# Moving the second stage's input normalization of 14 of 16 images out of the first stage, in a two-stage convolution kernel

## The reference, cut to what matters

```
x = x + L0_conv(gn(x))   # gn: each channel of each image to mean 0, variance 1
x = x + L1_conv(gn(x))
```

## Time and profile before

| | |
|---|---|
| median of 3 runs | 2269.34 us (2268.66 to 2269.86) |
| the profiled execution | 2273.27 us, of which the span of the profile is 2271.2 us |
| PE busy | 2145.7 us, 94% of the span |
| DVE, ACT, POOL busy | 77%, 63%, 23% |
| bytes moved by DMA | 248.21 MB, mean 109 GB/s |
| chain that ended last | 90% PE, 4% issue, 2% ACT, 2% DVE, 1% DMA |

### The profile page before, as it was taken

How to read it: one execution, slowest core, us unless ns; L and a number is a source line. 1 busy time by engine, 2 the same in 40 slices (tenths; PEclk the granted TensorE clock), 3 DMA queues, 4 the chain that set the end, 5 groups by cost and what they waited for, 6 DMA issues and landing times.

```text
span 2271.2 us, 101012 instructions
## 1 busy us (share of the span) xinstructions
PE 2145.7 (94%) x45303; PEld 1364.8 (60%) x45303; DVE 1741.6 (77%) x4186; ACT 1432.6 (63%) x2629; POOL 517.1 (23%) x323
## 2 busy tenths in 40 slices
PE   6888888977999999999999999999999999999997
PEld 3333333336666666666666666666666666666664
DVE  4666666645888888888888888788888888878886
ACT  3456655656666666666666666666666666666662
POOL 1000000000332222322222222233322322322222
PEclk9989988888999999999999999999999999999998
DMA  7688888876333333333333333333433333333312
GB/s 144 163 220 224 223 219 219 207 193 157 79 83 84 79 90 86 79 78 79 79 79 81 85 83 79 83 88 79 97 85 82 88 79 88 79 78 79 79 40 57
DMA packets 60386, 248.21 MB, mean 109 GB/s; under 512 B 12393, under 2 KB 12658, under 8 KB 53810
## 3 DMA queue, kind: packets, MB, share of 16 engines
q1 hardware_dynamic: 59954, 241.75, 44.9%
HBM read 139.99 MB, written 101.72 MB: 106 GB/s over the span
## 4 chain that ended last, share of the span: by engine, by line
PE 90%; issue 4%; ACT 2%; DVE 2%; DMA 1%; POOL 0%; SPq 0%; POOLq 0%; ACTq 0%
PE bank L590 24%; PE bank L530 17%; PE bank L575 10%; PE bank L662 10%; PE bank L650 9%; PE bank L603 7%; PE bank L683 6%; PE bank L612 5%; DVE arena L1215 2%; ACT arena L826 1%; ACT arena L731 1%; DMA arena<-tap_rows_in 1%; PE bank L544 0%; ACT arena L817 0%; PE bank L492 0%
## 5 line engine op out<-in xcount | busy, mean ns | idle before, releaser
L459 POOL TENSOR_TENSOR arena<-arena 128x8 f32<-128x8 f32 x256 | 492.8, 1925 | 1238.0 <-DVE arena L1125 1235.5
L590 PE MATMUL bank<-arena 128*64 128x512 f16 x4608 | 690.2, 394 | 0.0
L817 ACT ACTIVATE arena<-bank 100x512 f32<-100x512 f32 x1024 | 581.8, 599 | 110.1 <-PE bank L575 79.4
L575 PEld LDWEIGHTS bank<-arena 128*64 128x64 f16 (+1 forms) x8192 | 328.7, 104 | 232.6 <-issue 22.3
L530 PE MATMUL bank<-arena 32*32 32x508 f32 (+1 forms) x9216 | 384.2, 655 | 51.1 <-issue 36.4
L575 PE MATMUL bank<-arena 128*64 128x128 f16 (+1 forms) x8192 | 389.3, 220 | 18.0 <-DVE arena L1109 11.5
L1215 DVE TENSOR_TENSOR arena<-bank,arena 128x512 f32<-128x512 f32 x512 | 328.9, 684 | 48.2 <-issue 44.9
L826 ACT ACTIVATE arena<-bank,arena 128x256 f32<-128x256 f32 x512 | 261.3, 561 | 114.1 <-PE bank L603 111.2
L859 ACT ACTIVATE arena<-bank 128x512 f32<-128x512 f32 x256 | 152.9, 597 | 225.7 <-PE bank L650 223.9
L1144 DVE TENSOR_TENSOR arena<-arena,bank 128x512 f32<-128x512 f32 x256 | 174.8, 683 | 139.6 <-ACT arena L826 139.6
L650 PE MATMUL bank<-arena 100*32 100x128 f32 x8192 | 276.1, 275 | 1.3 <-ACT arena L817 1.3
(11 more groups left out here) (113 smaller groups left out, 1655.9 us busy)
## 6 DMA issues: line engine op xcount, KB each, us to landing
arena<-xn_d SPq DMA_DIRECT2D x128, 536.2 KB, 4.8
xn_d<-arena SPq DMA_DIRECT2D x130, 260.0 KB, 4.4
x_d<-arena SPq DMA_DIRECT2D x64, 512.0 KB, 8.1
arena<-x_d SPq DMA_DIRECT2D x128, 256.0 KB, 4.1
out<-arena SPq DMA_DIRECT2D x128, 256.0 KB, 2.7
arena<-x_in SPq DMA_DIRECT2D x32, 544.0 KB, 9.6
arena<-x_in SPq DMA_DIRECT2D x32, 528.0 KB, 9.4
arena<-spectra_in SPq DMA_DIRECT2D x1, 384.0 KB
```

The lines of the kernel that those rows point to most:

```text
L459: pool.tensor_tensor(tiny["rstd"][:, slot], tiny["var_eps"][:, slot], powers, ALU.pow).then_inc(s_root, 1)
L575: mm = pe.matmul(ring[g % len(ring)][low:high, 128 * i:128 * i + 128], w[:, first + low:first + high], hidden_w, start=True, stop=True)
L590: mm = pe.matmul(v_banks[chunk % 3][64 * s:64 * s + 64, :], v_w[:, 64 * tap:64 * tap + 64], at(xs[u % 3], row * WP + 32 * k + dx, [32 * WP ...
L817: act.activation(h_rows[0:WIN, :, first:first + 4], ring[g % len(ring)][0:WIN, :].rearrange("p (i c) -> p c i", i=4), ACT.Copy).then_inc(s ...
```

## The change

- **First stage.** Only images 0 and 1 (`EARLY`) are still normalized and stored to `xn_d` here. An image of `x` is loaded in eight DMAs of about 270 KB in place of four, `x2` is stored in eight of 256 KB in place of four of 512 KB, and each waits for a step of the convolution (`s_conv_step`): an x piece at steps 0, 2, ... 14, an x2 piece at steps 1, 3, ... 15. The `xs` of units 0 and 1 are loaded during the convolutions of images 14 and 15.
- **Second stage.** The other 14 images are normalized by halves: in units 0 to 27, `load_half` brings back rows of `x2_d`, ACT normalizes (`norm_half`) and rounds (`high_half`) within `spectral`, DVE computes the lost part (`low_half`), and `store_half` writes `xn_d`, two units ahead of the load that reads it. `xs` has two buffers, not three, and is loaded in two parts: rows 0 to 41 (`load_top`, four DMAs of 341 KB, each waited for) and rows 42 to 65 (`load_bottom`, four DMAs of 195 KB, waited for in pairs). `load_res` comes first in SP's unit and waits for each pair.

```diff
+    EARLY = 2
+    TOP = 42
+    HALVES = 2 * (NB - EARLY)
...
-            def load_x(b, quarters):
+            def load_x(b, part, q):
                 flat = x[b].rearrange("c h w -> c (h w)")
-                for q in quarters:
-                    first, last = max(q * (H // Q) - 1, 0), min((q + 1) * (H // Q) + 1, H)
-                    at_row = first - (q * (H // Q) - 1)
-                    sp.dma_start(xq[b % 3][32 * q:32 * q + 32, at_row * W:(at_row + last - first) * W],
-                                 flat[:, first * W:last * W]).then_inc(s_x_in[b % 3], 16)
-            def store_x2(b):
-                rows = x2_d[b].rearrange("ch (r c e) -> ch r c e", r=4, c=4)
-                for c in range(4):
-                    sp.dma_start(rows[:, :, c, :], x2[b % 3][32 * c:32 * c + 32, :].rearrange("p (r e) -> p r e", r=4)).then_inc(
-                        s_x2_out[b % 3], 16)
-            def store_xn(b):
-                for part, buf in ((0, xh), (1, xl)):
-                    rows = xn_d[b, part, :, 1:H + 1, :].rearrange("ch (r c y) w -> ch r c (y w)", r=4, c=4)
-                    for c in range(4):
-                        sp.dma_start(rows[:, :, c, :], buf[32 * c:32 * c + 32, :].rearrange("p (r e) -> p r e", r=4)).then_inc(
-                            s_xn_out, 16)
+                band_top, half_band = q * (H // Q) - 1, BAND // 2
+                first, last = max(band_top + half_band * part, 0), min(band_top + half_band * (part + 1), H)
+                sp.dma_start(xq[b % 3][32 * q:32 * q + 32, (first - band_top) * W:(last - band_top) * W],
+                             flat[:, first * W:last * W]).then_inc((s_x_first_in, s_x_second_in)[part][b % 3], 16)
+            def store_x2(b, c, half):
+                rows = x2_d[b].rearrange("ch (r c e) -> ch r c e", r=4, c=4)[:, 2 * half:2 * half + 2, c, :]
+                sp.dma_start(rows, x2[b % 3][32 * c:32 * c + 32, QPIX // 2 * half:QPIX // 2 * (half + 1)].rearrange(
+                    "p (r e) -> p r e", r=2)).then_inc(s_x2_out[b % 3], 16)
+            def store_xn(b, part, c):
+                rows = xn_d[b, part, :, 1:H + 1, :].rearrange("ch (r c y) w -> ch r c (y w)", r=4, c=4)
+                sp.dma_start(rows[:, :, c, :], (xh, xl)[part][32 * c:32 * c + 32, :].rearrange("p (r e) -> p r e", r=4)).then_inc(
+                    s_xn_out, 16)
...
-            def load_xs(u, paced=True):
-                b, half = divmod(u, 2)
+            def load_band(u, landed, first, last, g):
+                b, h = divmod(u, 2)
+                src = xn_d[b, g % 2, :, h * (H // 2) + first:h * (H // 2) + last, :].rearrange("c h w -> c (h w)")
+                sp.dma_start(xs[u % 2][32 * g:32 * g + 32, first * WP:last * WP], src).then_inc(landed[u % 2], 16)
+            def load_xs(u, landed, first, last, at_once):
                 for g in range(4):
-                    src = xn_d[b, g % 2, :, half * (H // 2):half * (H // 2) + HALF, :].rearrange("c h w -> c (h w)")
-                    sp.dma_start(xs[u % 3][32 * g:32 * g + 32, :], src).then_inc(s_xs_in[u % 3], 16)
-                    if paced:
-                        sp.wait_ge(s_xs_in[u % 3], 64 * (u // 3) + 16 * (g + 1))
+                    load_band(u, landed, first, last, g)
+                    if (g + 1) % at_once == 0:
+                        sp.wait_ge(landed[u % 2], 64 * (u // 2) + 16 * (g + 1))
+            def load_top(u, at_once):
+                load_xs(u, s_top_in, 0, TOP, at_once)
+            def load_bottom(u, at_once):
+                load_xs(u, s_bottom_in, TOP, HALF, at_once)
...
                 older, prev, later = image(b - 2), image(b - 1), image(b + 2)
-                if later is not None:
-                    if b > 0:
-                        sp.wait_ge(s_conv_mm, NCH * b)
-                    load_x(later, (0, 1))
-                if prev is not None:
-                    sp.wait_ge(s_x2_ready, NCH * b)
-                    store_x2(prev)
-                if later is not None:
-                    load_x(later, (2, 3))
-                if b == NB + 1:
-                    load_xs(1, paced=False)
-                if older is not None:
-                    sp.wait_ge(s_xl_ready, 4 * (older + 1))
-                    store_xn(older)
-                if b == NB - 3:
-                    sp.wait_ge(s_xn_out, 128 * (older + 1))
+                if b == NB - 2:
+                    sp.wait_ge(s_xn_out, 128)
                     sp.wait_ge(s_pads_stored, 32)
-                    load_xs(0, paced=False)
+                for piece in range(8):
+                    if 0 <= b < NB:
+                        sp.wait_ge(s_conv_step, 18 * b + 2 * piece + 1)
+                    if later is not None:
+                        if piece == 0 and b > 0:
+                            sp.wait_ge(s_conv_mm, NCH * b)
+                        load_x(later, piece // 4, piece % 4)
+                    if NB - 2 <= b < NB:
+                        u = b - NB + 2
+                        if piece < 4:
+                            load_band(u, s_top_in, 0, TOP, piece)
+                        else:
+                            load_band(u, s_bottom_in, TOP, HALF, piece - 4)
+                    if 0 <= b < NB:
+                        sp.wait_ge(s_conv_step, 18 * b + 2 * piece + 2)
+                    if prev is not None:
+                        if piece == 0:
+                            sp.wait_ge(s_x2_ready, NCH * b)
+                        store_x2(prev, piece % 4, piece // 4)
+                    if older is not None and older < EARLY:
+                        if piece == 0:
+                            sp.wait_ge(s_xh_ready, 2 * (older + 1))
+                        if piece == 4:
+                            sp.wait_ge(s_xl_ready, 4 * (older + 1))
+                        store_xn(older, piece // 4, piece % 4)
...
-            def load_res(u, pair):
-                for s in range(2):
-                    p0 = 64 * pair + 32 * s
-                    sp.dma_start(res[p0:p0 + 32, :].rearrange("p (l r) -> p l r", l=2),
+            def load_res(u):
+                for part in range(4):
+                    pair, s = divmod(part, 2)
+                    sp.dma_start(res[32 * part:32 * part + 32, :].rearrange("p (l r) -> p l r", l=2),
                                  image_rows(x2_d, u // 2, u % 2, pair, s)).then_inc(s_res_in, 16)
+                    if s == 1:
+                        sp.wait_ge(s_res_in, 64 * u + 16 * (part + 1))
...
-            sp.wait_ge(s_xn_out, 128 * NB)
-            load_res(0, 0)
-            load_res(0, 1)
+            def load_half(u):
+                b, h = divmod(u + 2 * EARLY, 2)
+                if u > 0:
+                    sp.wait_ge(s_half_low, 2 * u)
+                for g in range(4):
+                    first = (64 * h + 16 * g) * W
+                    sp.dma_start(half_x2[32 * g:32 * g + 32, :], x2_d[b, :, first:first + 16 * W]).then_inc(s_half_in, 16)
+                    if g in (1, 3):
+                        sp.wait_ge(s_half_in, 64 * u + 16 * (g + 1))
+            def store_half(u):
+                b, h = divmod(u + 2 * EARLY, 2)
+                done = 128 * EARLY + 128 * u
+                if u == 0:
+                    sp.wait_ge(s_half_pads, 2)
+                sp.wait_ge(s_half_low, 2 * (u + 1))
+                for part, buf in ((0, half_high), (1, half_low)):
+                    for g in range(4):
+                        first = 1 + 64 * h + 16 * g
+                        sp.dma_start(xn_d[b, part, :, first:first + 16, :].rearrange("c h w -> c (h w)"),
+                                     buf[32 * g:32 * g + 32, :]).then_inc(s_xn_out, 16)
+                        if g == 3:
+                            sp.wait_ge(s_xn_out, done + 64 * (part + 1))
+            for s in range(3):
+                sp.wait_ge(s_x2_out[s], 128 * len(range(s, NB, 3)))
+            sp.wait_ge(s_shift2, NB)
+            load_half(0)
             for u in range(1, LAST + 1):
+                sp.wait_ge(s_inverse_mm, 4 * u - 1)
+                load_res(u - 1)
+                if u > 1:
+                    load_bottom(u, 2)
+                if u <= HALVES:
+                    store_half(u - 1)
+                if u < HALVES:
+                    load_half(u)
                 if u < LAST:
-                    sp.wait_ge(s_hidden_mm, 32 * u + 1)
-                    load_xs(u + 1)
+                    sp.wait_ge(s_v_mm, 8 * u)
+                    sp.wait_ge(s_xn_out, 128 * EARLY + 128 * min(u, HALVES))
+                    load_top(u + 1, 1)
                 store_res(u - 1)
-                sp.wait_ge(s_inverse_mm, 4 * u + 3)
-                load_res(u, 0)
-                sp.wait_ge(s_res_in, 64 * u + 32)
-                load_res(u, 1)
+            sp.wait_ge(s_inverse_mm, 4 * LAST + 4)
+            load_res(LAST)
             store_res(LAST)
...
                                        start=i == 0, stop=i == 8)
+                        if r == 0 and c == 0:
```

(42 more changed lines are left out.)

75 lines of the change are left out of this document (39 added, 36 removed).

## The result

The changed kernel takes 2365.7 us (median of 4 runs, 2358.6 to 2381.7); the kernel before, on the same chip, 2269.0 (4 runs, 2267.6 to 2269.9). The ratio is 1.044, 95% interval 1.038 to 1.049: slower, as forecast, by 97 us where 168 were forecast. The profiled execution is one of 2358.6 us with a span of 2356.8, which is 85.6 more than the span of before.

What follows compares the result with a forecast made beforehand. SP's serial landings were to become the second stage's bound, above PE's 53.7 us a unit. Span 2271.2 - 70 (first stage) - 14 (transition) + 242 (SP) + 10 (clock) = 2439 us, median 2437 us, range 2335 to 2560 us.

Steps and rivals of the forecast that it cites:

- Part 4: Second stage, SP's order: sixteen groups waited for in turn outlast PE's 53.7 us a unit; delay 242 us at window 5.
- P: SP's summed group landings for one second-stage unit: 62.8 us, lowest 56.2, highest 72.6; each us is worth 26 us.
- from unit 28 on: End of the second stage: with the halves done, SP is quicker than PE again, without giving anything back.
- break-even: Rival for the second stage: P near its low end, 56.2 to 57.5, gives 2265 to 2300 us; chance 4%.
- Clock: Second stage: half clock after PE's stands makes window 5 to last v step nearly tie SP's half groups; 10 us in all.
- Part 1: First stage: fewer bytes in even pieces shorten an image to 24 us; net -70 us after two images' normalizing waits.
- Part 2: Transition between the stages: normalizing gone and both first `xs` landed; -14 us, bounds -5 and -20.
- Part 3: Second stage's added ACT and DVE normalizing: costs nothing as forecast; first `low_half` up to 1.2 us a unit otherwise.
- SP keeps up: Rival for the second stage: SP's unit does not exceed PE's, so 2185 to 2219 us, faster; chance 10%.
- Landings at the slow end: Rival for SP's second-stage groups: small pieces gain nothing, P = 68 to 72.6, 2570 to 2700 us; chance 8%.
- the first stage gains nothing: Rival for the first stage: x and x2 pieces keep queues full and PE's instructions late; 2507 us; chance 15%.

Runs made afterwards that it cites:

- e8: Changed kernel with only the second stage's residual stores (`store_res`) waited for in pairs, not one by one: 2267.6 us, ratio 0.9986 to the kernel before.
- e9: e8 with `load_bottom` of the next unit directly behind `load_top`, and `load_half`'s four loads waited for once: 2217.8 us, ratio 0.976 to the kernel before.
- e2: Changed kernel with `EARLY` = 14 in place of 2, so images 0 to 13 are normalized and stored in the first stage again: 2480.3 us, one run.
- e7: e2 with `load_bottom` of the next unit directly behind `load_top` in place of behind `load_res`: 2321.4 us, one run.
- e3: Changed kernel without the first stage's waits for convolution steps, x and x2 pieces issued as fast as SP can: 2391.9 us, one run.
- e10: e9 with the eight stores of `store_half` waited for once: 2191.3 us, ratio 0.965 to the kernel before.
- e12: e10 with both `low_half` behind the windows at the end of `spectral`: 2184.0 us, ratio 0.964 to the kernel before.
- e1: Changed kernel with the four loads of `load_top` issued together and waited for once: 2339.7 us, ratio 1.031 to the kernel before.
- e4: Changed kernel without every second-stage wait for a landing that no later SP instruction needs: 2271.9 us, ratio 1.0025 to the kernel before.
- e5: e8 with the loads of `load_top` issued and waited for in pairs: 2245.0 us, ratio 0.988 to the kernel before.

## Why the prediction was right, and where it was off

**The bound was named rightly.** Part 4 said that SP's landings, sixteen groups one after another, would pass PE's 53.7 us and that PE would meet them at window 5. The chain, the two equal numbers 59.74 and 59.87, the 215 us of waiting (some 240 forecast) and e8 and e9, in which the sum and the pass stay equal as they fall, show it. The second stage lost 178 us where 252 were forecast.

**The step that failed in size: P, 62.8 us.** It measured 59.7. Of the 3.1 too much, 1.9 are `store_half`, taken as a pair of 256 KB *loaded* (4.7 us a group) where a group of four stores of 130 KB lands in 3.75; the nearest row was not the pair of loads of equal bytes but the store of 256 KB at 3.0, plus its issues. Another 0.9 are `load_bottom`, 3.75 a pair where 4.2 was taken. `load_top` (14.7 for 14.8), `store_res` and the pairs of x2 were right within 0.5. At 26 passes the 2.9 between forecast and measured pass are 76 us, nearly all of the 74 by which the second stage's forecast was too high.

**A statement that was wrong: "from unit 28 on the halves are done and SP is quicker than PE again".** The passes of units 28 to 30 last 58.0, 58.7 and 59.3 us, and SP stands in them up to 15 us after the bottom rows have landed, waiting for the last v step (line 482; the 18.8 count from the last issue):

```profile
SPq L482 <- PE bank L659: 111.8, 30, 18.8
```

I had seen PE wait for SP at window 5 and SP wait for PE at the last v step, and called it nearly a tie within one unit; I had not added up the ring that the two waits close. e2 and e7 show it. Cost of the error: 3 passes of 5 us, 15 us. It also means that my break-even, a P of 56.2 to 57.5, was not the only condition: the ring's 58.4 stands above it.

**Clock: +10 us** for the two half groups against window 5 to the last v step. The pass exceeds the sum by 0.13 us, 3 us in all. The granted clock is 0.96 in the second stage, and the slices show it as 9 tenths, not 8. The slower matmuls cost PE 2 us a unit, but no time of the unit: the pass is SP's sum.

The four add up: 252 - 76 - 7 + 15 = 184, against 178.

**Part 1: -70 us.** Measured -70.9. The size is right, the reason half so: it was forecast that the stage gains because an image's bytes fall *and* come in even pieces. The two stretches divide the gain: 46 us are PE's busy time for the same 9400 matmuls (406.8 to 360.6, the clock from 0.90 to 0.98), 25 are idle time, in which "issue" went from 38.8 us to 0.6 and the waits for ACT from 14 to 26. "Issue" is nearly gone with the old bytes in pieces (e2, 0.8 us, where PE's long waits for ACT may have a part in it), and with fewer bytes without the pacing (e3, 3.0). No run had the old order and size of x and x2 with the new place of normalizing, so how the two share the 71 us stays open; the pacing alone is 4 to 7.

**Part 2: -14 us.** Measured -19.5, near the bound of -20.

**Part 3: nothing.** Right as the forecast put it: with SP as the bound no wait of PE for this work shows. For the case in which PE binds, up to 1.2 us a unit was given for the first `low_half`; in e10 against e12, from window to window, a unit lasts 54.0 and 53.9, so it is some 0.1 to 0.2 us a unit.

**A row that was read wrongly, without effect:** SP's waits for the residual of 19.4 us count from the last issue of `load_xs` and so hold its landing, some 5 us. SP worked some 39 us of a unit before, not 34, and had less to spare. The forecast was added up from the groups and does not rest on it.

**The rivals.** "SP keeps up" was given 10% and the page's rule with it: the Trainium skill, "DMA: Bandwidth & Descriptors", on two cost components, made 47 us of SP's unit. It is 59.7. The page gives this formula for DMAs issued by way of gpsimd, and these are issued from SP; the prediction did not say so. For the 341 KB load it makes 2.8 us and the trace has 3.6; the measurement decides. "Landings at the slow end" fell with 3.6 to 3.9 us for the smaller loads; "the first stage gains nothing" fell with 388.9. What the rival had in size, 2185 to 2219 us once SP keeps up, is where e9 to e12 came out, 2184 to 2218, after two or three of SP's waits and the place of `load_bottom` were changed.

**What stays open.** Why loads of 341 KB in flight together delay PE, while four loads of 256 KB (e9), pairs of other loads and bursts of stores do not, was not taken apart. Rows, bytes and direction differ between them, and so does the place in the unit, a rival that no run tests: `load_top` runs beside the short inverse matmuls (all but two of the 87 gaps in e1, e4 and e5 stand on their three lines), where PE starts some 60 matmuls and weight loads a us, against 23 in the rest of the unit, and so uses up its instruction packets faster.

## What to carry to other kernels

When spare time of a queue is spent, add up its program for one period, group by group with measured landings of the same direction, and compare it with the bound engine's period; then look for the ring too, from the landing through the engine and back to the issue that waits for it, since it binds without any of its members being busy. Which waits are between transfers, and which transfer stands behind which, can be worth more than their bytes: here one wait a pair instead of one a store gave back the whole loss, and one group moved gave 159 us. Waits for landings on the issuing queue are not only cost, as e1, e4 and e5 show: take them out from the stores and small loads first, and look at "issue" on PE after each.

## What the runs showed of the hardware that was not expected

- PE waits for its own instructions when large loads are in flight together, far from full DMA queues in the mean. Gaps of PE over 0.4 us with "issue" as their cause, after 560 us: 1 us with the 341 KB loads one at a time (the changed kernel; 0, 2 and 1 in e8, e9 and e10), 25 us with two (e5), 53 us with four (e1), 48 us with four and no other wait for a landing either (e4); the DMA share from 600 to 1900 us is 0.44, 0.50 and 0.47 in the changed kernel, e12 and e1, so the mean share does not tell them apart. The granted clock of that stretch is 0.98 in e1 and 1.00 in e5 and e12; it is 0.96 in the changed kernel, whose PE stops some 4 us a unit for rows.
- PE's instructions come by DMA too: the page of the profile has a queue of kind instruction, with 5.85 MB in 357 packets in each of these kernels. PE goes on 1.2 to 1.6 us after such a packet has landed, in each of the 87 gaps of e1, e4 and e5.
- Loads and stores of equal size do not land in equal time: of pairs of 256 KB in e8, a store lands in 3.4 us and a load in 4.0 (medians); a store alone takes 2.6. Eight stores of 130 KB with one wait take 5.9 us (e10), with two waits 7.8 (e9).
